# Variance kept in PSUM between its two operations, and one-column operations written with two scalars, in a fused norm, projection and gate kernel

## The reference

```python
def _L0_conv_ref(x, W, b):
    u = jnp.mean(x, axis=1, keepdims=True)
    var = jnp.var(x, axis=1, keepdims=True, ddof=1)
    s = jnp.sqrt(var)
    n_x = (x - u) / (s + EPS)
    n_x = jnp.einsum('bchw,oc->bohw', n_x, W) + b[None, :, None, None]
    return x * n_x
...
x = x + _L0_conv_ref(_gn(x), L0_conv_W, L0_conv_b)
```

## Time and profile before

| | us |
|---|---|
| median of 3 runs | 1960.63 |
| lowest and highest | 1960.15, 1963.23 |
| the profiled execution, whole | 1957.16 |
| its span in the trace | 1955.4 |
| DVE busy | 1803.2 |
| PE busy | 1713.4 |
| POOL busy, ACT busy | 1460.6, 1440.7 |
| granted TensorE clock, mean | 0.992 |

### The profile page before, as it was taken

One profiled execution on the slowest core, in us unless ns is written; L12 is line 12 of the kernel. 1 busy time (PEld: TensorE's weight loads), 2 busy tenths in 40 slices (PEclk: granted clock), 3 DMA queues, 4 the chain that ended last, 5 costly groups with the idle time before them and its releaser, 6 DMA issues.

```text
span 1955.4 us, 67613 instructions
## 1 busy us (share of the span) xinstructions
PE 1713.4 (88%) x28706; PEld 922.9 (47%) x28706; DVE 1803.2 (92%) x2120; ACT 1440.7 (74%) x2498; POOL 1460.6 (75%) x1684
## 2 busy tenths in 40 slices
PE   0079997999889998999989999899988999899997
PEld 0045554555445554455545554455544555455553
DVE  5669999999999998999989998999989999898988
ACT  5598885888768885788858888588876888544442
POOL 0077877878778886788868787787877888688885
PEclk9989999999999999999999999999999999999999
DMA  9989998999989998999989999899998999854775
GB/s 379 390 308 337 388 377 291 402 378 377 337 293 415 372 385 322 338 396 373 387 303 378 372 385 350 304 406 373 380 346 310 401 364 384 315 196 185 270 258 218
DMA packets 184188, 671.63 MB, mean 343 GB/s; under 512 B 20688, under 2 KB 21072, under 8 KB 183888
## 3 DMA queue, kind: packets, MB, share of 16 engines
q1 hardware_dynamic: 110160, 398.85, 55.0%
q10 hardware_dynamic: 73728, 268.47, 34.6%
HBM read 398.80 MB, written 268.44 MB: 341 GB/s over the span
## 4 chain that ended last, share of the span: by engine, by line
PE 47%; DVE 27%; issue 9%; DMA 9%; POOL 3%; SPq 2%; ACT 2%; POOLq 0%; ACTq 0%; DVEq 0%
PE proj_ps L734 28%; PE sums_ps L722 10%; DVE scaled L632 9%; PE factor_ps L708 9%; DMA tiles<-x 6%; DVE tiles L645 6%; DVE bn L676 4%; DVE bn L677 4%; DMA out<-tiles 3%; SPq L408 2%; POOL tiles L441 1%; POOL tiles L452 1%; DVE var L651 1%; ACT unused L509 1%; DVE gn L580 1%
## 5 line engine op out<-in xcount | busy, mean ns | idle before, releaser
L734 PE MATMUL proj_ps<-scaled,w_t 128*32 128x512 f32 x8192 | 992.3, 602 | 0.1
L452 POOL TENSOR_SCALAR tiles<-tiles,out_shift 128x1024 f32<-128x1024 f32 x512 | 576.8, 1127 | 228.6 <-DVE tiles L645 214.9
L645 DVE SCALAR_TENSOR_TENSOR tiles<-proj_ps,gate_shift,tiles 128x1024 f32<-128x1024 f32 x512 | 643.2, 1256 | 46.4 <-PE proj_ps L734 46.0
L441 POOL TENSOR_SCALAR tiles<-tiles,norm_scalars 128x1024 f32<-128x1024 f32 x512 | 618.6, 1208 | 58.0 <-DMA tiles<-x 57.2
L509 ACT ACTIVATE unused<-tiles,bn 128x1024 uint8<-128x1024 f32 x560 | 636.5, 1137 | 2.5 <-issue 1.7
L632 DVE TENSOR_TENSOR scaled<-tiles,factor_ps 128x1024 f32<-128x1024 f32 x512 | 618.4, 1208 | 6.1 <-PE factor_ps L708 3.8
L524 ACT ACTIVATE squares<-tiles 128x1024 f32<-128x1024 f32 x512 | 539.0, 1053 | 99.1 <-POOL tiles L441 74.2
L708 PE MATMUL factor_ps<-pieces,pick_sb 128*128 128x128 bf16 x4096 | 319.8, 221 | 130.5 <-DVE scaled L632 111.5
L722 PEld LDWEIGHTS sums_ps<-tiles,const_sb 128*32 128x32 f32 x8192 | 245.6, 111 | 317.9 <-issue 283.7
L734 PEld LDWEIGHTS proj_ps<-scaled,w_t 128*32 128x32 f32 x8192 | 214.7, 109 | 365.0 <-issue 311.5
L708 PEld LDWEIGHTS factor_ps<-pieces,pick_sb 128*128 128x128 bf16 x4096 | 232.5, 98 | 245.8 <-DVE scaled L632 164.5
(11 more groups left out here) (56 smaller groups left out, 679.9 us busy)
## 6 DMA issues: line engine op xcount, KB each, us to landing
tiles<-x SPq DMA_DIRECT2D x760, 512.0 KB, 9.7
out<-tiles ACTq DMA_DIRECT2D x512, 512.0 KB, 6.9
const_sb<-const SPq DMA_DIRECT2D x1, 193.5 KB, 2.3
scaled<-w SPq DMA_DIRECT2D x1, 64.0 KB, 2.1
scaled<-ident SPq DMA_DIRECT2D x1, 64.0 KB, 2.1
pick_sb<-pick SPq DMA_DIRECT2D x1, 8.0 KB, 2.2
bias_sb<-bias SPq DMA_DIRECT2D x1, 0.5 KB, 2.3
```

The costliest lines, as they stand in the source:

```text
L441: nc.gpsimd.tensor_scalar(place(s), place(s), norm_scalars[:, 0:1], norm_scalars[:, 1:2], ALU.add, ALU.mult).then_inc(normed, 1)
L452: nc.gpsimd.tensor_scalar(place(s), place(s), 1.0, out_shift[:, 0:1], ALU.mult, ALU.add).then_inc(finished, 1)
L645: nc.vector.scalar_tensor_tensor(out=place(s), in0=proj_ps[:, s % 2, :], scalar=gate_shift[:, 0:1], in1=place(s), op0=ALU.add, op1=ALU.mul ...
L734: mm = nc.tensor.matmul(proj_ps[q:q + 32, s % 2, h:h + BANK], w_t[:, q:q + 32], scaled[:, s % 2, h:h + BANK], start=True, stop=True)
```

## The change

`var_ps(s)` is the third 128-column part of the set's bank in `sums_ps`, which nothing used. The first operation of the variance (L651) writes there, and the second (L655) reads it there and writes `var` in SBUF as before. PE's two waits that protected the bank are now for `var_done`, the second operation's semaphore, since the bank is read until then. In `gn_scalars` six operations of the form `scalar_tensor_tensor` on one column, of which the third operand was a tensor of one column, are written as `tensor_scalar` with two scalars; operands, order and arithmetic are the same. No instruction is moved, added or removed on any engine. In the new kernel L651 and L655 are L649 and L653, and lines from there on stand 2 lower.

```diff
+        def var_ps(s):
+
+            return sums_ps[:, s // SPLIT % 2, 2, :]
...
-                    then(nc.vector.scalar_tensor_tensor(out=cell(5), in0=cell(4), scalar=cell(4), in1=cell(1),
-                                                        op0=ALU.mult, op1=ALU.add))
-                    then(nc.vector.scalar_tensor_tensor(out=cell(4), in0=cell(4), scalar=bn_part, in1=cell(2),
-                                                        op0=ALU.mult, op1=ALU.subtract))
-                    then(nc.vector.scalar_tensor_tensor(out=cell(5), in0=cell(5), scalar=bn_part, in1=cell(3),
-                                                        op0=ALU.mult, op1=ALU.add))
-
-                    then(nc.vector.scalar_tensor_tensor(out=cell(5), in0=cell(4), scalar=cell(4), in1=cell(5),
-                                                        op0=ALU.mult, op1=ALU.subtract))
+                    then(nc.vector.tensor_scalar(cell(5), cell(4), cell(4), cell(1), ALU.mult, ALU.add))
+                    then(nc.vector.tensor_scalar(cell(4), cell(4), bn_part, cell(2), ALU.mult, ALU.subtract))
+                    then(nc.vector.tensor_scalar(cell(5), cell(5), bn_part, cell(3), ALU.mult, ALU.add))
+
+                    then(nc.vector.tensor_scalar(cell(5), cell(4), cell(4), cell(5), ALU.mult, ALU.subtract))
...
-                    then(nc.vector.scalar_tensor_tensor(out=cell(7), in0=cell(7), scalar=cell(7), in1=cell(5),
-                                                        op0=ALU.mult, op1=ALU.subtract))
+                    then(nc.vector.tensor_scalar(cell(7), cell(7), cell(7), cell(5), ALU.mult, ALU.subtract))
...
-                    then(nc.vector.scalar_tensor_tensor(out=cell(11), in0=cell(8), scalar=cell(10), in1=cell(9),
-                                                        op0=ALU.mult, op1=ALU.add))
+                    then(nc.vector.tensor_scalar(cell(11), cell(8), cell(10), cell(9), ALU.mult, ALU.add))
...
-                        nc.vector.scalar_tensor_tensor(out=var[:, :], in0=sum_sq[:, :], scalar=-1.0 / P,
+                        nc.vector.scalar_tensor_tensor(out=var_ps(step - LAG_VAR), in0=sum_sq[:, :], scalar=-1.0 / P,
                                                        in1=sums_of(step - LAG_VAR)[:, 1, :], op0=ALU.mult, op1=ALU.add)\
                             .then_inc(var_sum_done, 1)
                         dve.wait_ge(var_sum_done, ready)
-                        nc.vector.tensor_scalar(var[:, :], var[:, :], TINY, 1.0 / (P - 1), ALU.max, ALU.mult)\
+                        nc.vector.tensor_scalar(var[:, :], var_ps(step - LAG_VAR), TINY, 1.0 / (P - 1), ALU.max, ALU.mult)\
                             .then_inc(var_done, 1)
...
                 if s % SPLIT == 0 and (before or s >= 2 * SPLIT):
-                    pe.wait_ge(var_sum_done, b * sets + s // SPLIT - 1)
+                    pe.wait_ge(var_done, b * sets + s // SPLIT - 1)
...
-                            pe.wait_ge(var_sum_done, b * sets + (sets - 1))
+                            pe.wait_ge(var_done, b * sets + (sets - 1))
```

## The result

The changed kernel takes 1923.4 us (median of 5 runs, 1922.92 to 1930.45), the kernel before 1960.63: a ratio of 0.9826, with a 95% interval of 0.98 to 0.9852. That is 37 us less where 28 were forecast (1932.5, range 1920 to 1949). The profiled execution took 1922.92 us against 1957.16.

The account below looks back on a forecast made before the run. PE was taken as the floor, with DVE adding in certain steps. Savings of 20.4 + 4.5 + 0.5 + 9.3 = 34.7 us, less 6.5 given back, made 28 us net: 1932.5 us, range 1920 to 1949.

Parts of the forecast that it names:

- The bound: Whole kernel: PE is the floor, and DVE lengthens only certain steps; a 3.62 us step becomes 3.28, 4.10 stays.
- The steady part: The 60 steps of 3.62 us behind two statistics items become 3.28 with a faster clamp, 20.4 us saved.
- The first steps: A batch's first step, where PE idles 0.87 us behind clamp, statistics item and scale: 6 x 0.75 = 4.5 us saved.
- The clamp: L655 reading PSUM takes 0.29 us in place of 1.07 where POOL held it, 0.78 us of DVE saved per held place.
- The two-scalar forms: One-column operations in gn_scalars with two column scalars take 0.25 us, between bounds of 0.15 and 0.29.
- the prediction's sign: What the trace should show on DVE: busy time down about 87 us from the clamp and 12 from the scalars.
- What is given back: Late loads in a batch's last slots and longer transfer queues on DMA take back 6.5 us of the gain.
- The transitions apart from first steps: Between batches, the one-column operations and the clamp on DVE become shorter, 9.3 us saved over seven transitions.
- falls more often: Rival: PE's clock falls more often after longer idle times at late loads; with 36 more, 1973 us; 2%.
- the fast rival: PE's clock falls less often: the five slow projections between batches go and nothing is given back, 1920 us; 8%.
- The held clamp: Rival: the clamp on DVE stays held by POOL because its output is in SBUF; 5 to 9 us saved, 1954; 4%.
- the DMA rival: Loads of the last slots are paced by transfers, so DMA takes the steady gain back; 10 us saved, 1950; 12%.

## Why the prediction was right, and where it was off

**The bound.** "PE is the floor, and DVE adds to it in certain steps only" held to the hundredth. 61 pairs of 4.10 and 3.28 us are in the trace, none of 3.62. The steady part gave 20.3 us against 20.4; the run without the clamp and the one with one more show both sides of the spare time, nothing gained and nothing lost.

**The first steps.** 4.21 became 3.44 us, 6 x 0.77 = 4.6 against 4.5.

**The clamp.** 0.291 us against 0.29 taken from L562. Writing PSUM cost L649 about 5 ns. The two-scalar forms took 0.273 us against 0.25. By the sums of durations the clamps fell by 86 us and the columns by 11; the 15 us that went to L665 were not foreseen. DVE's busy time, which counts overlapping operations once, fell by 75.9, where the prediction's sign had 87 and 12. The 15 us cost nothing in the steady part, which came out as forecast; in a kernel bound by DVE they would have eaten about a sixth of the gain, an estimate from 15 of 97.

**What is given back.** This is the term that was mis-sized: 6.5 us subtracted, nothing found. POOL's waits for loads are 57.7 us against 57.2 (56.4 when the changed kernel was run again), while the median load takes 10.0 us to land, against 9.7. The rows fit loads of the last slots that follow a store and thus the compute, so that what was gained before them moved them as a whole; this reading was not tested by a run:

```profile
POOL tiles L445 <- DMA tiles<-x: 57.7, 41, 3.3
```

The transitions apart from first steps gave 8.5 us where 9.3 less 6.5 were forecast. That figure alone proves little, since against the trace with the waits alone, 298.6 us in place of 303.9, it would be 3. The whole does: with the 34.7 us gross of the prediction, a measured 34.3 in span and 35 and 37 between medians, leaving the term out would have been right.

**The clock.** The rival "falls more often" was given 2% and named the right mechanism in the wrong kernel: it is what the variance part does alone in most executions, 14.8 us of transitions. The change as a whole escapes it because its second part shortens the idle time in front of the step behind the scalars to 1.73 us. I had priced the column operations by their length, 0.45 us for L609; the run with that one put back shows 10 us. A further slow projection was priced at 1.0 to 1.5 us; behind the scalars it lengthened the step by 1.6 to 1.7 (4.89 to 4.96 in place of 3.27). The prediction counted five slow projections between batches in the trace of before. There are six, of 2.95 to 3.39 us. Two traces of the changed kernel have 6 and 5, the three with an old column form and the new clamp 12, 11 and 12. So they did not go down, and the fast rival did not happen either.

**The held clamp and the DMA rival** are ruled out by the rows of L653 and of L445.

## What to carry to other kernels

When a busy engine has gaps of its own in the length of its steps, find which steps it sets, by the starts of the other engine's work, and price an edit per such step: 86 us of DVE time were worth 25 here, and a single instance in the trace where the disturbance was absent gave the number beforehand. Where an operation in SBUF is sometimes more than four times its shortest length, see whether it ends with an operation of GpSimd, as all 120 did here; one end in PSUM freed this one, and a part of the wait turned up at the next operation with two SBUF inputs, so look for that one. Small operations in front of a TensorE that idles about 2 us should be counted with the clock that they may cost, and two parts of a change should be measured alone as well as together.

## What the runs showed of the hardware that was not expected

- A `tensor_scalar` of 128 x 128 with its input in PSUM and output in SBUF takes 290 to 294 ns beside a busy GpSimd, and 294 to 296 the other way round; with both ends in SBUF it took 226 to 1087, and the held ones ended 77 to 83 ns after GpSimd's operation.
- Operations of DVE that don't wait for one another overlap: three of 280 to 290 ns each occupied it for 0.59 us.
- One-column operations of 214 ns with one column scalar take 273 with two, and none of these forms was held.
- A one-column operation that is held for half a us can cost 2 us: with 2.18 us of idle time in front of a step, a projection took 3.46 us, and with 1.74 us it took 1.92. In other places 2.17 us were harmless, one of them in the same trace.
